# Query and key parts in DRAM with the chunk of 512 tokens outside parts and depth, and their pieces loaded over seven steps

## The reference

```python
xn = _layernorm(x, axis=-1)
# attention, T = 1024, H = 16, D = 16
q = einsum('btc,hcd->bhtd', xn, Wq) + bq;  k = ... Wk, bk;  v = ... Wv, bv
scores = einsum('bhtd,bhsd->bhts', q, k) * D ** -0.5
probs = softmax(scores + causal, axis=-1)
y = einsum('bhts,bhsd->bhtd', probs, v) -> (B, T, 256);  attn = y @ Wo + bo
# experts, 8 of 256 x 256 (gate, up) and 256 x 256 (down)
topk_logits, selected = top_k(xn @ Wr, 2);  w = softmax(topk_logits)
ffn = sum over e of w_e * ((clip(silu(xn @ Wg[e]), -7, 7) * (xn @ Wu[e])) @ Wd[e])
return x + attn + ffn
```

## Time and profile before

| | us |
|---|---|
| median of 3 runs (437.99 to 438.84) | 438.12 |
| the profiled execution, time | 438.36 |
| its span, from the first to the last instruction | 436.4 |
| TensorE busy | 412.3 |
| VectorE busy | 332.0 |
| ScalarE busy | 222.4 |
| POOL busy | 196.5 |

### The profile page before, as it was taken

The page is one execution under the profiler, slowest core; times in us unless marked ns, Lnnn a source line. Parts: engine busy times, 40 slices in busy tenths (PEclk is TensorE's granted clock), DMA queues, the critical chain, the costliest instruction groups (busy, mean ns, idle before and its releaser), DMA issues.

```text
span 436.4 us, 8151 instructions
## 1 busy us (share of the span) xinstructions
PE 412.3 (94%) x2755; PEld 246.4 (56%) x2755; DVE 332.0 (76%) x1043; ACT 222.4 (51%) x511; POOL 196.5 (45%) x223
## 2 busy tenths in 40 slices
PE   8998979989999999999799999999999999999993
PEld 8585414655364465566547567565667476556332
DVE  6827999999989859775287866789396988881795
ACT  1563362334646566545164355456555445646970
POOL 5331266576064187256474265415655255313320
PEclk9999979999999999999899999999999999999996
DMA  7289896788067089235954239805595336110782
GB/s 228 82 218 194 289 200 211 226 285 282 3 160 174 1 252 279 75 110 170 214 168 156 103 110 249 248 24 182 164 235 178 136 101 194 24 26 6 236 271 72
DMA packets 40372, 71.33 MB, mean 163 GB/s; under 512 B 5893, under 2 KB 30598, under 8 KB 40332
## 3 DMA queue, kind: packets, MB, share of 16 engines
q0 software_dynamic: 9360, 39.99, 29.1%
q1 hardware_dynamic: 27132, 26.76, 25.0%
q10 hardware_dynamic: 3840, 4.08, 3.7%
HBM read 55.85 MB, written 15.60 MB: 164 GB/s over the span
## 4 chain that ended last, share of the span: by engine, by line
PE 68%; DVE 21%; DMA 4%; issue 4%; ACT 1%; POOL 1%; SPq 0%; ACTq 0%; DVEq 0%; POOLq 0%
PE psum L1293 14%; PE psum L1330 14%; PE psum L1254 11%; PE psum L1273 11%; PE psum L1339 8%; DVE psum L981 7%; DVE mxa L984 4%; PE psum L1209 3%; PE psum L1185 3%; PE psum L1312 3%; DMA bqk<-in_bqk 2%; PE psum L1320 2%; DMA xg<-xn_rows,token 2%; DVE resid L953 1%; DMA x<-in_x 1%
## 5 line engine op out<-in xcount | busy, mean ns | idle before, releaser
L894 ACT ACTIVATE probs<-psum 128x512 f32<-128x512 f32 (+1 forms) x320 | 151.1, 581 | 40.9 <-PE psum L1273 40.3
L981 DVE CUSTOM_DVE_ANT_0 psum<-psum,maskrow 128x128 f32<-128x128 f32 (+3 forms) x256 | 121.4, 506 | 14.3 <-PE psum L1254 14.0
L1254 PE MATMUL psum<-packk,packq 96*128 96x512 bf16 (+3 forms) x384 | 94.2, 328 | 3.3 <-DVE mxb L981 1.2
L1273 PE MATMUL psum<-packq,packk 99*128 99x512 bf16 (+3 forms) x384 | 91.0, 330 | 3.3 <-ACT probs L894 2.1
L984 DVE TENSOR_REDUCE mxa<-psum 128x1 f32<-128x512 f32 x128 | 87.7, 685 | 5.4 <-PE psum L1254 5.3
L1293 PE MATMUL psum<-probs,v 128*32 128x512 f32 (+3 forms) x768 | 75.7, 503 | 1.0 <-POOL probs L821 0.9
L1254 PEld LDWEIGHTS psum<-packk,packq 96*128 96x128 bf16 x384 | 35.1, 97 | 56.1 <-issue 15.9
L821 POOL TENSOR_SCALAR_AFFINE_SELECT probs<-probs 128x512 f32<-128x512 f32 (+1 forms) x48 | 41.2, 863 | 44.8 <-ACT probs L894 44.7
L1273 PEld LDWEIGHTS psum<-packq,packk 99*128 99x128 bf16 x384 | 33.4, 98 | 42.7 <-issue 10.5
L788 POOL DMA_INDIRECT xg<-xn_rows,token x39 | 37.7, 967 | 38.9 <-PE psum L1320 27.4
L806 POOL DMA_INDIRECT expert_rows<-wvr,slots x39 | 39.3, 1008 | 31.8 <-ACT wvr L914 17.2
(11 more groups left out here) (120 smaller groups left out, 457.8 us busy)
## 6 DMA issues: line engine op xcount, KB each, us to landing
qk_parts<-stage SPq DMA_DIRECT2D x24, 256.0 KB, 3.9
stage<-expert_rows SPq DMA_DIRECT2D x16, 256.0 KB, 4.1
packq<-qk_parts SPq DMA_DIRECT2D x16, 192.0 KB, 5.4
packk<-qk_parts SPq DMA_DIRECT2D x14, 192.0 KB, 5.8
x<-in_x SPq DMA_DIRECT2D x4, 512.0 KB, 6.2
packq<-qk_parts SPq DMA_DIRECT2D x16, 128.0 KB, 6.0
xn_rows<-probs ACTq DMA_DIRECT2D x4, 512.0 KB, 14.7
out<-x SPq DMA_DIRECT2D x16, 128.0 KB, 3.0
```

Source lines behind the costliest of these rows:

```text
L894: act.activation(probs[:, g % RING, h, 0:width], psum[:, bank, 0:width], ACT.Exp, scale=SCALE)\
L981: ins = dve.tensor_tensor_reduce(out=chunk, in0=chunk, in1=maskrow[:, BANK - width:], scale=1.0, scalar=NEG, op0=ALU.add, op1=ALU.max, acc ...
L1254: pe.matmul(psum[:, bank, 0:width], packq[0:MAXROW, u % SLOTS, i // HALF, h, P * (i % HALF):P * (i % HALF + 1)], packk[0:MAXROW, u % SLOTS ...
L1273: ins = pe.matmul(psum[:, bank, at:at + width], packk[0:KROWS, u % SLOTS, j // HALF, h, P * (j % HALF):P * (j % HALF + 1)], packq[0:KROWS, ...
```

## The change

In DRAM `qk_parts` had the axes (queries or keys, group of 8 heads, part, depth, head, 2048 tokens). It now has (queries or keys, group, chunk of 512 tokens, part, depth, head, 512 tokens). For a load the four heads of one part and depth and chunk were four pieces of 1 KB, 4 KB apart; they are now one row of 4 KB. In SBUF they already stood in one row of 4 KB, and the loads now name them so. The stores write the same 1 KB rows to their new places.

For units 3 to 7 the pieces no longer all wait for step 9 of unit u-3. `step_before_load` gives each piece a step of its own: with k = 3c + r, step 9 of unit u-3 plus floor(3k/2) steps, that is step 9 of unit u-3 and then steps 0, 2, 3, 5 and 6 of unit u-2. The planner's `after` and SP's wait take that step.

```diff
+LOAD_EVERY = 3
+def step_before_load(u, c, r):
+    return NS * (u - SLOTS + 1) - 1 + (c * len(RUNS) + r) * LOAD_EVERY // 2
...
         for c in range(2):
-            after = [("SP", ("store", 4 * b + 2 * (g // 2) + c))]
-            if u >= SLOTS:
-                after += [("PE", ("s", NS * (u - SLOTS + 1) - 1, UH - 1))]
             for r in range(len(RUNS)):
+                after = [("SP", ("store", 4 * b + 2 * (g // 2) + c))]
+                if u >= SLOTS:
+                    after += [("PE", ("s", step_before_load(u, c, r), UH - 1))]
...
-        qk_d = nc.dram_tensor("qk_parts", [2, 2, PARTS, HD, H // 2, N], BF16).ap()
+        qk_d = nc.dram_tensor("qk_parts", [2, 2, N // BANK, PARTS, HD, H // 2, BANK], BF16).ap()
...
-                    cols = slice(T * b + BANK * n, T * b + BANK * (n + 1))
-                    sp.dma_start(qk_d[:, grp, part, :, :, cols].rearrange("o d h t -> (d h) o t"),
+                    sp.dma_start(qk_d[:, grp, T // BANK * b + n, part, :, :, :].rearrange("o d h t -> (d h) o t"),
...
-                    wait_filled(sp, ("s", NS * (u - SLOTS + 1) - 1, UH - 1))
+                    wait_filled(sp, ("s", step_before_load(u, c, r), UH - 1))
...
-                    src = qk_d[op, grp, first[op]:first[op] + length, :, h0:h0 + UH, T * b + BANK * c:T * b + BANK * (c + 1)]
-                    sp.dma_start(pack[row:row + HD * length, u % SLOTS, c, :, :],
-                                 src.rearrange("r d h t -> (r d) h t")).then_inc(pack_in[u % SLOTS][c], 16)
+                    src = qk_d[op, grp, T // BANK * b + c, first[op]:first[op] + length, :, h0:h0 + UH, :]
+                    sp.dma_start(pack[row:row + HD * length, u % SLOTS, c, :, :].rearrange("p h t -> p (h t)"),
+                                 src.rearrange("r d h t -> (r d) (h t)")).then_inc(pack_in[u % SLOTS][c], 16)
```

More of the change, by code:

```diff
@@ L849, in load_first_k @@
                 row, _, first, length = RUNS[r]
-                act.dma_start(packk[row:row + HD * length, 0, c, :, :],
-                              qk_d[1, 0, first:first + length, :, 0:UH, BANK * c:BANK * (c + 1)].rearrange("r d h t -> (r d) h t"))\
+                act.dma_start(packk[row:row + HD * length, 0, c, :, :].rearrange("p h t -> p (h t)"),
+                              qk_d[1, 0, c, first:first + length, :, 0:UH, :].rearrange("r d h t -> (r d) (h t)"))\
                     .then_inc(pack_in[0][c], 16)
```

## The result

The changed kernel takes 440.86 us (median of 12 runs, 439.37 to 442.08), the kernel before 438.31 (median of 12, 436.79 to 440.16): a ratio of 1.0055 [1.0037, 1.0072], slower by some 2.4 us where 5.4 us less was forecast. The profiled execution took 440.55 us with a span of 438.6 (before: 438.36 and 436.4), so the two traces can be set against each other directly.

The account below looks back on a forecast made before the run. TensorE, busy 412.3 of 436.4 us, was taken as the bound, leaving idle time and low clock to win. Gains of 2.8 (burst), 1.5 (clock) and 1.2 (start) sum to 5.5: 438.36 - 5.5 = 432.9 us, range 430.3 to 436.8.

Parts of the forecast that it names:

- The rows of 4 KB at the start: Start, near 36 us: fewer load packets free ScalarE's held store and end VectorE's idle time; gain 1.2 us, 0 to 2.8.
- rival 3: Gather at 205 us still waits behind the first piece's 4 KB packets; 437.2 or 438.4 us, chance 0.11.
- The burst taken apart: Gather near 205 us: with two of twelve loads left, TensorE's stall falls from 3.26 to 0.42 us; gain 2.8, 1.7 to 3.3.
- the upper residual: Gather near 205 us: two loads wholly ahead of it, 384 KB at 352 GB/s = 1.1 us, leave 1.5 us of wait.
- The clock: After the stall, 212.8 to 216.2 us: no fall to 1.2 GHz expected; gain 1.5 us, between 0 and 1.7.
- The new waits and the stores in their new places: Load gates of units 3 to 7: all new waits costed at 0, with 4.7 us to spare for the negated maxima.
- the signs that I had given for the change itself: Unit 5's loads leave in six pairs over some 45 us; 1 KB packets fall by about 9,000.
- rival 4: Loads could meet gathers at thirty moments, not five; two new stalls of 4.8 us each give 442.5 us, chance 0.07.
- Rival 1: Start: loads as slow as before, ScalarE's queue held as before, only spreading gains 4.3 us; 434.1 us, chance 0.22.
- Rival 2: Gather near 205 us: 1.5 to 2 us of wait remain and the clock still falls; 435.7 us, chance 0.10.

Follow-up runs that it names:

- e2: Kernel before (1 KB rows, old layout) with only the new spread gates: 437.69 us, ratio 0.9994.
- e5: Changed kernel (4 KB rows) with every load gate one step later: 438.54 us, ratio 1.0013 to the kernel before.
- e11: Kernel before (1 KB rows, old layout) with spread gates, each one step later than in the change: 434.43 us, ratio 0.9926.
- e3: Changed kernel with a 512-byte gap behind each run of 512 tokens in DRAM, so loads have 1 KB rows again: 436.58 us, ratio 0.9956.
- e4: Changed kernel with the planner putting unit 1's twelve loads behind unit 0's negated maxima: 444.58 us, ratio 1.014 to the kernel before.
- e7: e6 with every load gate one step later, rows of 1 KB: 441.12 us, ratio 1.007 to the kernel before.
- e6: e2 with unit 1's twelve loads placed by hand directly behind unit 0's negated maxima in SP's list: 443.71 us, ratio 1.0111 to the kernel before.
- e1: Changed kernel (4 KB rows, new layout) with the old gate for every piece: 445.04 us, ratio 1.0162 to the kernel before.
- e10: Changed kernel (4 KB rows), gates one step later, loads of units 1 and 2 placed by hand behind stores in SP's list: 432.86 us, ratio 0.9891.

## Why the prediction was wrong

The forecast was 432.9, the range 430.3 to 436.8, and 0.07 on slower. By its own steps:

**The rows of 4 KB at the start: wrong in sign.** The term was 1.2 us of gain, "between 0 and 2.8". It was a loss of 3 to 4 us at the end of the kernel (after against e2: 3.2; e5 against e11: 4.1; after against e3: 4.3). The step that failed: "fewer packets should clear the queues in front of the store". ScalarE's issue was held for 6.65 us and not for less than 4.27, and the number of packets was hardly a limit: the loads' rate went only from 162 to 170. The earlier trace rows already hinted at it (64 KB landing no sooner than 192 KB). What the length of packets does set is how two queues share a DMA engine, and there the long ones win against the 1 KB stores of ScalarE's queue. That the longer rows lengthen the hold is shown (e3, 4.19 us; after, 6.65), and that unit 1's loads must stand there for it (e4, 0.37); that the shared turns are what lengthens it is argued. I wrote in rival 3 that the longer rows would get a larger share, and applied it to the gather alone. It was to be applied to every transfer beside such loads, above all where I had just placed a gain: the lower bound of 0 left out the mechanism that I had myself named.

**The burst taken apart: right mechanism, mis-sized.** Forecast 3.26 to 0.42 us, gain 2.8; measured 3.26 to 2.37 in after and e2, gain 0.9, outside the bounds of 1.7 to 3.3. The term that failed is the upper residual, 384 KB at 352 GB/s = 1.1 us: 352 was the sum of the loads, the weight fetch and other traffic before the stall, and the loads' own rate was the other row of the same group, 168. 384 KB at that rate are 2.3 us, where the runs give 1.9 (2.37 less the 0.46 that stay without the two loads). The estimate of 0.42 us for a gather with no load ahead was good: 0.21 to 0.61 once the two loads were moved (e5, e7 to e11). What I wrote of POOL in the stall, that it was only issuing, was not quite so: 0.7 of its 3.07 us were a sum of vectors. Nothing hangs on it.

**The clock: half right, and unsettled.** In the middle of after there is no fall to 0.50, as forecast, and the lag shrinks by 1.6 us there, where the term was 1.5. But it didn't come as I had argued: 2.37 us of idle time remain, more than the 1.5 that I had allowed for it, and in repeated runs of the kernel the mean clock goes from 0.967 to 0.981, so other executions may have the fall. So the right size of this term is in part luck. The idle times of 2.37 (e2) and 2.41 (e3) were followed by a fall, those of 2.37 (after), 2.29 (e6) and 2.56 (e4) were not. So the length of that idle time alone doesn't decide it, and I can't say what does. Before's own trace had a warning: behind 1.90 us of idle time at 56.72 the clock is at 0.50 from 59.2 to 66.1. At the start the forecast of no change was wrong: 3.92 us of idle time were followed by a fall to 0.50 that before doesn't have.

**The new waits and the stores in their new places: 0, right.** TensorE has no wait for a load or for negated maxima in after. All that it waited for from a DMA, as its list of waits has it:

```profile
PE psum L1325 <- DMA xg<-xn_rows,token: 2.7, 2, 2.4
...
PE psum L1190 <- DMA bqk<-in_bqk: 1.3, 1, 1.3
```

That is the gathers and the start's input, which answers to the earlier trace rows. e3, with the new places, the new gates and short rows, is faster than before (0.9956 [0.9936, 0.9976]). The first piece and its gather apart, the signs that I had given for the change itself came true: SP's loads of unit 5 go out in six pairs (over 55 us), and the packets in all fall by 9,216 (those of 1 KB alone by 12,288, not by the 9,000 that I had written). The thirty moments of rival 4 made no new stall of size: beside the old one, 2.37 us, the gathers cost 0.3.

**The rivals.** Rival 4's range, 439 to 443, holds the number, by luck: its cause, new stalls at gathers, isn't there. None had the mechanism. Rival 1 has the right rate of the loads and the wrong consequence, since it let the queue be held "as before". Rival 2 comes nearest to the middle (2.37 where it said 1.5 to 2). Rival 3 has the right rule at the wrong place (and took the gather's packets for 1 KB): at the gather, e2 with 1 KB rows waits as long as after. The port rule cited against the gain (the Trainium skill, "SBUF — State Buffer", section "Door 1: The DMA port swizzle") asked for loads that are no faster for longer rows, and 162 against 170 GB/s agrees with that; no run here varied the partitions of a piece, so the ports as the cause weren't tested. Its sum of 4.3 us of gain missed all the same.

**The sum, redone from the runs.** Gates, by e2: 437.69 - 438.22 = -0.5. Long rows behind them, by after against e2: +3.2. That these come to the 2.55 measured is no check, since e2 stands in both. The parts do not simply add: with the old gates the long rows and their new places cost 445.04 - 438.22 = 6.8 us, so the spread gates are worth 4 us to the kernel with long rows and 0.5 to the one with short. Part of that is the idle time in the middle, 3.47 us in e1 and 2.37 in after; the rest lies in where the clock fell (e1 has its four falls, at 45, 62, 103 and 219) and isn't taken apart further.

**What is open.** Why ScalarE's issue of the fourth store is held until about 40 or 43 us stays open. A full queue behind starved stores would be a reading, but before's hold ends a microsecond ahead of the first packet of any store. Shown is only that it takes 4.2 to 4.3 us beside short loads, 6.7 beside long ones and 0.37 with unit 1's loads away. Why after has a stretch at 0.50 near 102 us, as e1, e4, e6, e7 and e11 have at 100 to 109, is open too: after's TensorE is busy for 2.09 of the 3 us in front of it, the rest is short waits of at most 0.4 us.

## What to carry to other kernels

Before you lengthen a transfer's rows, list what else is queued at the same moment and with what rows: here the stores beside the longer rows fell to a third of their bandwidth, and such a loss is paid by whoever waits for them. Price a transfer by a window in which it runs alone, never by one in which several run; and when a burst in front of a critical transfer is taken apart, ask first what the piece that stays in front still costs. A transfer that nobody needs for another 55 us (unit 1's, issued at 31 to 36 and first used at 91) should not be issued beside one that holds an engine: placing such loads elsewhere was worth 5.7 us to the kernel with long rows (e5 to e10).

## What the hardware showed that I had not expected

- With full DMA engines, loads of 16 to 48 partitions moved 162 GB/s in rows of 1 KB and 170 in rows of 4 KB. With stores of 1 KB rows from a second queue beside them, the total was twice that in the first case (319) and 1.2 times in the second (208), and stores alone moved some 380. A DMA share above 1 thus says nothing about how many more bytes another queue could move.
- A DMA issue can hold an engine's whole queue: 6.65 us for one `dma_start` that takes 0.37 with unit 1's loads away, and the copies behind it on ScalarE wait with it.
- A packet need not be a row: gathers of 1 KB rows went as packets of 4 KB (34 packets for 0.14 MB), the loads and stores of the start as one packet per row.
- The start varies from run to run of otherwise equal code: TensorE's wait for the small input `bqk` before its first products was 0.42 us in before and 1.3 in after. With differences of 2 us between kernels, moments in two single traces can be compared only with that in mind (e4 and e11 waited 2.5 and 2.1 us there), and verdicts come from the repeated runs side by side.
